# Gate and up products of an RWKV-7 layer issued as four column tiles of 32 output rows

## What is computed

```python
wg, wu, wd = (w / 127 for w in (w_gate, w_up, w_down))     # int weights, (768,256), (768,256), (256,768)
gate = einsum('bsd,hd->bsh', xn, wg)
up   = einsum('bsd,hd->bsh', xn, wu)
h    = silu(gate) * up
g    = silu(einsum('bsh,dh->bsd', h, wd))
out  = x + rwkv7(xn) * g
```

## Time and profile before

| what | value |
|---|---|
| median of 3 runs | 1608.94 us (1607.33 to 1612.72) |
| span of the profiled execution | 1603.4 us |
| PE busy | 1520.5 us, 95% of the span, 20288 instructions |
| DVE (VectorE) busy | 1243.6 us, 78% |
| ACT (ScalarE) busy | 1069.5 us, 67% |
| POOL (GpSimd) busy | 354.6 us, 22% |

### The profile page before, as it was taken

One profiled execution on the slowest core, in us unless ns is written; L12 is line 12 of the kernel. 1 busy time (PEld: TensorE's weight loads), 2 busy tenths in 40 slices (PEclk: granted clock), 3 DMA queues, 4 the chain that ended last, 5 costly groups with the idle time before them and its releaser, 6 DMA issues.

```text
span 1603.4 us, 48245 instructions
## 1 busy us (share of the span) xinstructions
PE 1520.5 (95%) x20288; PEld 1064.9 (66%) x20288; DVE 1243.6 (78%) x2661; ACT 1069.5 (67%) x1889; POOL 354.6 (22%) x362
## 2 busy tenths in 40 slices
PE   3699999999999999999999999999999999999887
PEld 1366767576676757667676676757667675766765
DVE  2968787787878878887887878778787887888643
ACT  3758586685857758685775858668585775768512
POOL 3121402313040131302213140231304013130201
PEclk9799999999999999999999999999999999999999
DMA  4011110301212021111202111030121202111020
GB/s 149 14 25 29 33 34 16 62 18 32 43 25 47 16 55 25 33 34 24 56 16 39 42 34 34 16 62 19 33 42 25 48 16 55 25 33 34 12 56 28
DMA packets 251430, 57.85 MB, mean 36 GB/s; under 512 B 223696, under 2 KB 250704, under 8 KB 251088
## 3 DMA queue, kind: packets, MB, share of 16 engines
q1 hardware_dynamic: 241936, 41.95, 13.9%
q10 hardware_dynamic: 9280, 12.81, 2.2%
HBM read 36.38 MB, written 18.35 MB: 34 GB/s over the span
## 4 chain that ended last, share of the span: by engine, by line
PE 92%; DVE 3%; ACT 2%; issue 1%; POOL 0%; DMA 0%; SPq 0%; ACTq 0%; DVEq 0%; POOLq 0%
PE bank L534 23%; PE chunk L380 15%; PE bank L544 11%; PE bank L509 8%; PE bank L664 4%; PE chunk L642 3%; PE chunk L614 3%; PE chunk L589 3%; PE chunk L598 2%; PE bank L485 2%; PE bank L380 2%; PE bank L517 2%; PE bank L479 2%; PE chunk L628 2%; DVE VU L981 1%
## 5 line engine op out<-in xcount | busy, mean ns | idle before, releaser
L1325 POOL TENSOR_TENSOR SF<-ST,CT 128x256 f32<-128x256 f32 x128 | 99.7, 779 | 728.8 <-DVE ST L1211 728.8
L534 PE MATMUL bank<-xT,wg 128*128 128x256 f32 x768 | 197.2, 391 | 14.2 <-DVE VU L981 13.5
L534 PE MATMUL bank<-xT,wu 128*128 128x256 f32 x768 | 207.3, 395 | 0.0
L544 PE MATMUL bank<-wd,hT 128*128 128x256 f32 x768 | 176.8, 383 | 1.9 <-DVE hT L1171 1.9
L534 PEld LDWEIGHTS bank<-xT,wg 128*128 128x128 f32 x768 | 136.3, 189 | 57.6 <-DVE VU L981 24.1
L544 PEld LDWEIGHTS bank<-wd,hT 128*128 128x128 f32 x768 | 143.3, 190 | 29.3 <-issue 7.2
L534 PEld LDWEIGHTS bank<-xT,wu 128*128 128x128 f32 x768 | 135.1, 188 | 34.8 <-issue 14.5
L380 PE MATMUL chunk<-KS,W 128*128 128x512 f32 x320 | 149.6, 598 | 0.3 <-ACT gT L719 0.3
L509 PE MATMUL bank<-qpad,KS 128*64 128x32 f32 x4096 | 141.2, 226 | 4.0 <-DVE KE L1143 4.0
L887 ACT ACTIVATE Y<-chunk 32x256 f32<-32x256 f32 x256 | 96.3, 376 | 70.9 <-PE chunk L598 67.0
L509 PEld LDWEIGHTS bank<-qpad,KS 128*64 128x64 f32 x4096 | 130.7, 141 | 14.1 <-issue 9.0
(11 more groups left out here) (156 smaller groups left out, 3231.3 us busy)
## 6 DMA issues: line engine op xcount, KB each, us to landing
smalls<-in_x SPq DMA_DIRECT2D x32, 256.0 KB, 3.1
Y<-in_x SPq DMA_DIRECT2D x32, 256.0 KB, 3.0
out<-fsil ACTq DMA_DIRECT2D x32, 256.0 KB, 2.6
scrA<-AM SPq DMA_DIRECT2D x64, 64.0 KB, 1.9
hat<-scrB SPq DMA_DIRECT2D x32, 128.0 KB, 3.1
hat<-scrF SPq DMA_DIRECT2D x32, 128.0 KB, 3.1
KE<-scrA SPq DMA_DIRECT2D x64, 32.0 KB, 2.2
scrT<-KE SPq DMA_DIRECT2D x16, 128.0 KB, 1.7
```

Of the source, the lines that this page charges most:

```text
L534: q = pe.matmul(o[:, TT_ * n2:TT_ * n2 + TT_], w[:, h, 128 * (n + n2):128 * (n + n2) + 128], x_now[:, h], start=(h == 0), stop=(h == NH - 1))
L544: q = pe.matmul(o[:, 256 * m:256 * m + 256], hT[:, n, 128 * m:128 * m + 128], wd[:, n, :], start=(n == 0), stop=(n == NF - 1))
L1325: pool.tensor_tensor(SF[:, :, :, :], ST[:, :, :, :], fade[:, c].unsqueeze(3).to_broadcast([128, B, NH, N]), ALU.mult).then_inc(*faded.up)
```

## The change

Each matmul of the gate and up products is split by its output rows into four with 32 weight columns each; each writes 32 partitions of the same bank and reads the same 256 columns of xn. The loop over the four stands inside the one over h. The weights, the banks, the yields and the increment stay as they are.

```diff
                             for n2 in range(2):
                                 for h in range(NH):
-                                    q = pe.matmul(o[:, TT_ * n2:TT_ * n2 + TT_], w[:, h, 128 * (n + n2):128 * (n + n2) + 128],
-                                                  x_now[:, h], start=(h == 0), stop=(h == NH - 1))
+                                    for p0 in range(0, 128, 32):
+                                        q = pe.matmul(o[p0:p0 + 32, TT_ * n2:TT_ * n2 + TT_],
+                                                      w[:, h, 128 * (n + n2) + p0:128 * (n + n2) + p0 + 32],
+                                                      x_now[:, h], start=(h == 0), stop=(h == NH - 1))
                                 if n2 == 0:
                                     yield f"{name}{b}{n}"
```

## The result

| | before | changed |
|---|---|---|
| median of 9 runs on the same chip | 1608.80 us (1604.66 to 1612.94) | 1617.15 us (1613.91 to 1619.60) |
| ratio, 95% interval | | 1.0045 (1.0023 to 1.0066): 3.7 to 10.6 us slower |
| span of the profiled execution | 1603.4 us | 1615.7 us |

The kernel became slower by 7.2 us by the ratio, 8.35 by the medians. The two spans differ by 12.3 us, which is more. The time of a run with a recorded span is 1.4 to 1.5 us above that span, so of the 5.5 us between before's span and its median, which the text ahead of the prediction put down to what lies outside the span, some 4 are there because this execution was a quick one. The changed kernel's profiled execution lay at its median. The forecast time is not touched by this: it adds the change to the median.

What follows compares the result with a forecast made beforehand. TensorE, busy 95% of the span, was taken as the bound. Terms -18.1 + 5.4 + 17.6 + 5.4 + 1.5 = +11.8 us on the 1608.9 median gave 1620.7 us; likeliest case 1613 to 1630, chance 70%; range 1611 to 1662, 83%.

Steps and rivals of the forecast that it cites:

- Four at a time: Gate and up: four column tiles over the same rows run at once, a set costing 0.216 us; extra cost 0.
- the streams of 1941 and 2604 us: Rivals: gate and up tiles run two at a time, +332 us, chance 6%, or all in turn, +995, chance 2%.
- The 1 ns a set: Gate and up: each set of four tiles takes 1 ns longer than one full-array instruction, +1.5 us in all.
- Loads in the open: Rival: each gate or up set waits 25 ns for a 32-column load, +38 us on top, about 1659; chance 6%.
- Loads in turn: Rival: where nothing hides them, the four tiles' loads run one after another, +34 us, 1643 us; chance 7%.
- The entry from a tiled product: At 221 gate or up runs behind a tiled product, the narrower first load saves 82 ns each, -18.1 us.
- skew: Gate and up: four tiles start some 7 ns apart, adding 0.02 us at each of 269 runs, +5.4 us.
- The entry from a full-array product: At 48 gate or up runs behind a full-array product, new gap and load cost 0.113 us each, +5.4 us.
- Leaving for a full-array product: At 94 gate or up runs followed by a full-array product, new gap and mostly first load, +17.6 us together.
- the rival with nothing due at these borders: Changes between full-array and column tiles cost nothing, entries from row-tiled products still save: -11.2 us, faster; chance 4%.
- Which waits absorb: PE waits twice a section, before gate (0.9 us) and L420 (some 0.4); absorption costed at nothing, at most 6 us.

Runs made afterwards that it cites:

- beside_full: Against the kernel before, only the 110 gate and up runs with a full-array product before or behind them split into column tiles; 1624.23 us, ratio 1.0103.
- alone: Against the kernel before, only the 159 gate and up runs between tiled products on both sides split into column tiles; 1601.71 us, ratio 0.9949.
- all_products: Against the kernel before, all 1760 matmuls of L380, L479, L485, L534, L544 and L664 split into column tiles; 1609.67 us, ratio 1.0022.

## Why the prediction was right, and where not

It said 1620.7 us, 0.7% slower; it is 1617.15, 0.45% slower. By the profile, step by step:

- **Four at a time: right.** Sets of four go on at 0.216 us (four units in line cost their streaming plus the entry, 3.60 = 3.46 + 0.14), so the streams of 1941 and 2604 us fall (both had left out the 11.8 us of the other terms, which changes nothing here). The 1 ns a set was not there: in line, sets take 216 ns, as before; the term is 0 and not +1.5.
- **Loads in the open (1659): wrong**, by the same row. The Trainium skill (TensorE: Matmul & The Clock Gate, Part 3, "What overlaps and what doesn't") lets a load overlap only where the row group differs; here four tiles over all rows load for the next set while they run, and no time shows. Trace and rule differ, and the trace decides. Loads in turn (1643) falls by the first records of a run: those of all four tiles last 403 to 404 ns, 26 more than 378, and start 7 ns apart, and a lone unit fell from 1.06 to 1.00.
- **The entry from a tiled product: right.** 26 ns of load instead of 105 and a skew of 20 make 0.06 saved; measured 1.06 to 1.00. The price of a load by width, 23 by halving, was 26.
- **The entry from a full-array product: right.** 0.09 + 0.023 + skew = 0.13; measured 0.86 to 1.00.
- **Leaving for a full-array product: right.** 0.195 forecast; measured 0.18 to 0.20 at L380 and the wo product. That the rival with nothing due at these borders (1597.7) fell is shown by beside_full, which is 10.84 us longer in ten periods and splits only units that have such a border.
- **Which waits absorb: wrong in part.** The prediction's "PE waits twice in a section" was incomplete. There is a third place, L485, where TensorE waited for ScalarE, too short to be a row in the list of waits: a piece "issue" of 0.07 us in the chain, and the 0.48 us between two starts. It takes back 0.14 us a period where work ahead of it is longer (beside_full), and takes the gain where it is shorter (alone). The lone unit ahead of the L454 products saved nothing either: those products started no earlier. The L401 wait in front of gate stayed at 0.9 us in every kernel, as said, since it moves with TensorE's own work.
- **The size.** The sum was 11.8 us for the kernel. Ten periods say 10.1 for 16 tiles, the two sets of runs 7.2 and 9.0 with intervals of 3.7 to 10.6 and 6.3 to 11.6. In the commonest period the forecast's 11.8 / 16 = 0.74 stands against 0.79. The mean is 0.63, because four of before's ten periods were longer than its commonest (0.7 us of them are waits at L628, which the changed kernel has not). The 1.5 us of the sets was too much, and the saving was too large by about as much: one lone unit a period without any (0.06) and 0.03 lost at L485 make 1.4 in 16. So the terms at the borders were right, that these two errors cancel is luck, and the sum came out high against the mean by before's irregular periods, which no term had. The runs say 1 to 3 us less than the periods, but their intervals (3.7 to 10.6, 6.3 to 11.6) hold the 10.1; a difference could lie in the first and last stretches, where the clock is not at its upper level all the time. It was not settled.

## What to carry to other kernels

Where an array's tilings alternate, price the borders and not the products: here a split into column tiles cost nothing as such, saved load at a border that is there anyway, and paid gap and load at each new one. So split only the products whose neighbours are tiled; done that way, the same edit gains 0.5% instead of losing it. And before moving a product out of a wait, look at what it covers for the wait behind it.

## What the runs showed of the hardware that was not expected

- The load that shows behind a change of tiling goes by the columns, 105, 53 and 26 ns for 128, 64 and 32, once for all tiles that load side by side.
- The starts of four tiles are 7 ns apart when they are neighbours in the program and 13 ns when each tile's two matmuls are; a matmul that waits for its own tile didn't hold up those of other tiles (a lone unit of 1.02 us).
- A VectorE record of 1.43 us became 5.02 beside GpSimd's work in three periods of all_products, where in the others a GpSimd record of 1.2 became 2.3. The wait of 2.63 us that it caused was followed by 6.5 us or more at the lower clock each time. Such a period is 5.6 us longer, as much as the whole change costs in nine.
